# Scatters of edge weights and edge counts spread over more blocks, and paced by the block beside them, in a network of graph and feed-forward layers

## The reference, cut to what matters

```python
# layer 2, graph: a sum weighted by edge_val
h = x @ weight_l
agg = segment_sum(edge_val[:, None] * h[edge_col], edge_row, 3125)
out = agg + bias_l + x @ weight_r + bias_r
# layer 3, graph, twice: a sum with norm = dinv[s] * dinv[d]
h = x @ W
out = segment_sum(h[s] * norm[:, None], d, 3125) + b
```

## Time and profile before

| | us |
|---|---|
| median of 3 timed runs | 4196.15 |
| lowest and highest of them | 4191.04, 4196.79 |
| span of the profiled execution | 4599.8 |

### The profile page before, as it was taken

How to read it: one execution, slowest core, us unless ns; L and a number is a source line. 1 busy time by engine, 2 the same in 40 slices (tenths; PEclk the granted TensorE clock), 3 DMA queues, 4 the chain that set the end, 5 groups by cost and what they waited for, 6 DMA issues and landing times. The chain is left out here.

```text
span 4599.8 us, 50306 instructions
## 1 busy us (share of the span) xinstructions
PE 3306.7 (72%) x14651; PEld 2298.0 (50%) x14651; DVE 1956.1 (43%) x5106; ACT 1198.3 (26%) x3021; POOL 2015.7 (44%) x2028
## 2 busy tenths in 40 slices
PE   3888887177878888348833686798054968999796
PEld 2666665066444455136621454454043744448685
DVE  5554458403666667899833123100044443211201
ACT  2444441023222222148831111000021212103231
POOL 4666656710555555644464554345635421000121
PEclk8666668588888888669966798899576989998898
DMA  4444441002766667147711322543031234332112
GB/s 159 154 161 160 154 166 36 1 1 67 201 194 197 193 192 203 50 141 242 237 58 60 103 88 73 186 150 100 0 124 41 65 96 164 144 108 83 49 37 76
DMA packets 278411, 542.57 MB, mean 118 GB/s; under 512 B 61218, under 2 KB 187110, under 8 KB 277508
## 3 DMA queue, kind: packets, MB, share of 16 engines
q1 hardware_dynamic: 199876, 396.17, 25.5%
q0 software_dynamic: 78272, 143.18, 11.5%
HBM read 370.70 MB, written 168.47 MB: 117 GB/s over the span
## 5 line engine op out<-in xcount | busy, mean ns | idle before, releaser
L1235 PE MATMUL bank<-layer_gnn_h_nodes,layer_gnn_s_onehot_t 128*128 x1664 | 546.3, 456 | 105.1 <-issue 62.7
L144 POOL DMA_INDIRECT edge_weights<-shares,share_cell x416 | 460.2, 1106 | 269.6 <-DMA edge_weights<-shares,share_cell 158.2
L1187 POOL DMA_INDIRECT layer_gnn_s_rows<-gat_rows,src_cols x416 | 401.1, 964 | 370.5 <-DMA kept_rows<-layer_gnn_s_rows 209.7
L134 POOL DMA_INDIRECT edge_counts<-repeats,count_cell x416 | 419.8, 1009 | 270.7 <-DMA edge_counts<-repeats,count_cell 166.0
L496 POOL DMA_INDIRECT layer_gnn_sum_rows<-xn_rows,src_cols x416 | 423.9, 1019 | 199.9 <-issue 102.9
L1235 PEld LDWEIGHTS bank<-layer_gnn_h_nodes,layer_gnn_s_onehot_t 128*128 128x128 f32 x1664 | 316.4, 211 | 201.9 <-issue 127.8
L555 PE MATMUL bank<-layer_gnn_sum_onehot,layer_gnn_sum_rows 128*128 128x128 f32 x1664 | 370.9, 387 | 63.9 <-issue 46.5
L1484 PE MATMUL bank<-layer_gnn_w_onehot,layer_gnn_w_part 128*128 128x128 f32 x1664 | 293.8, 305 | 121.7 <-issue 67.8
L555 PEld LDWEIGHTS bank<-layer_gnn_sum_onehot,layer_gnn_sum_rows 128*128 128x128 f32 x1664 | 322.0, 282 | 116.7 <-issue 81.4
L1484 PEld LDWEIGHTS bank<-layer_gnn_w_onehot,layer_gnn_w_part 128*128 128x128 f32 x1664 | 226.0, 198 | 189.7 <-issue 96.9
L2594 PE MATMUL bank<-layer_gnn_b_weights,xn_nodes 128*128 128x400 f32 x768 | 261.2, 503 | 65.6 <-DMA layer_gnn_b_weights<-edge_weights 65.6
(11 more groups left out here) (611 smaller groups left out, 5565.2 us busy)
## 6 DMA issues: line engine op xcount, KB each, us to landing
kept_rows<-layer_gnn_s_rows SPq DMA_DIRECT2D x104, 512.0 KB
layer_gnn_w_rows<-kept_rows SPq DMA_DIRECT2D x104, 512.0 KB
edge_weights<-layer_gnn_sum_zeros SPq DMA_DIRECT2D x56, 800.0 KB
layer_gnn_b_weights<-edge_weights SPq DMA_DIRECT2D x56, 800.0 KB
layer_gnn_gcn_sum_counts<-edge_counts SPq DMA_DIRECT2D x50, 896.0 KB, 4.4
layer_gnn_s_dst_across<-in_dst_row SPq DMA_DIRECT2D x104, 256.0 KB
edge_counts<-layer_gnn_w_no_edges SPq DMA_DIRECT2D x25, 896.0 KB
layer_ffn_e_w<-in_l1f_w SPq DMA_DIRECT2D x16, 1024.0 KB
```

The lines of the kernel that those rows point to most:

```text
L134: nc.gpsimd.indirect_dma_start(g.counts, bass.IndirectOffsetOnAxis(ap=g.cell[:, t:t + 1].bitcast(U32), axis=0), g.repeats[:, t:t + 1], Non ...
L144: nc.gpsimd.indirect_dma_start(g.weights, bass.IndirectOffsetOnAxis(ap=g.share_cell[:, t:t + 1].bitcast(U32), axis=0), g.shares[:, t:t + 1 ...
L1187: nc.gpsimd.indirect_dma_start(rows[:, t % U, :], None, htable, bass.IndirectOffsetOnAxis(ap=g.srcc[:, t:t + 1].bitcast(U32), axis=0)).the ...
L1235: last = nc.tensor.matmul(g.ps[4 + t % 4][:, 0:D + HEADS], onehot_t[:, t % 4, k, :], hflat[:, ds(w * AW + (k * AW + HEADS), D + HEADS)], s ...
```

## The change

`LANES` becomes 4, and both helpers get a number `ahead`: scatter t waits for t − ahead to have landed. It is 2 as before unless given. A new helper, `place_weights_beside`, also makes each scatter wait for a semaphore of the block: tile t of lo to hi waits until it stands at `first + (t - lo) * steps // (hi - lo)`. The tables become longer.

| block | weights before | weights now | counts before | counts now |
|---|---|---|---|---|
| mod_ffn | 20 + 140 | 20 (one in flight) + 78 paced by `hidden` | | |
| gat_front | | 10 paced by `evicted` | | |
| edge_softmax | 20 | 46 (one in flight) | | |
| weighted_sum | 236 | 190 paced by `summed` | | |
| sw_gate | | 8 (one in flight) | | |
| sw_route | | 10 (one in flight) | 20 | |
| experts, layer 1 | | 54 | 96 | 40 |
| weighted_products | | | 240 | 270 (four in flight) |
| layer2_sums | | | | 20 (one in flight) |
| mo_gate | | | 30 | 16 (one in flight) |
| mo_route | | | 30 | 16 (one in flight) |
| experts, layer 2 | | | | 54, one a tile |

```diff
-LANES = 2
+LANES = 4
...
+def landed(eng, lanes, t):
+
+    eng.wait_ge(lanes[t % LANES], 16 * (t // LANES + 1))
...
+def place_weights(nc, g, pool, lo, hi, ahead=2):
 
     for t in range(lo, hi):
-        lane = g.weights_in[t % LANES]
-        if t >= LANES:
-            pool.wait_ge(lane, 16 * (t // LANES))
+        if t >= ahead:
+            landed(pool, g.weights_in, t - ahead)
         nc.gpsimd.indirect_dma_start(g.weights, bass.IndirectOffsetOnAxis(ap=g.share_cell[:, t:t + 1].bitcast(U32), axis=0),
-                                     g.shares[:, t:t + 1], None).then_inc(lane, 16)
+                                     g.shares[:, t:t + 1], None).then_inc(g.weights_in[t % LANES], 16)
+
+
+def place_weights_beside(nc, g, pool, lo, hi, signal, first, steps):
+
+    for t in range(lo, hi):
+        pool.wait_ge(signal, first + (t - lo) * steps // (hi - lo))
+        place_weights(nc, g, pool, t, t + 1)
...
-PLACED = (160, 180)
-COUNTED = (20, 116, 356, 386)
+PLACED = (20, 98, 108, 154, 344, 352, 362)
+COUNTED = (40, 310, 330, 346, 362)
...
-                place_weights(nc, g, pool, 20, PLACED[0])
+                place_weights_beside(nc, g, pool, PLACED[0], PLACED[1], hidden, 5, NF * (ROWS // G))
...
+                place_weights_beside(nc, g, pool, PLACED[1], PLACED[2], evicted, 1, NT)
...
-            place_weights(nc, g, pool, PLACED[0], PLACED[1])
+            place_weights(nc, g, pool, PLACED[2], PLACED[3], ahead=1)
...
-            place_weights(nc, g, pool, PLACED[1], ET)
+            place_weights_beside(nc, g, pool, PLACED[3], PLACED[4], summed, 1, ET)
...
-                    place_counts(nc, g, pool, COUNTED[0] + per * e, COUNTED[0] + per * (e + 1))
+                    place_weights(nc, g, pool, *share(PLACED[6], ET, e))
+                    place_counts(nc, g, pool, *share(0, COUNTED[0], e))
...
+                    if t < ET - COUNTED[4]:
+                        place_counts(nc, g, pool, COUNTED[4] + t, COUNTED[4] + t + 1)
...
-            place_counts(nc, g, pool, COUNTED[1], COUNTED[2])
+            place_counts(nc, g, pool, COUNTED[0], COUNTED[1], ahead=4)
...
+        @block.gpsimd
+        def _(pool):
+            place_counts(nc, g, pool, COUNTED[1], COUNTED[2], ahead=1)
```

More of the change, by code:

```diff
@@ L125, in _, with place_counts @@
             nc.tensor.matmul(g.ps[0][:, 0:ET], g.ones[0:1, :], df[0:1, :], start=True, stop=True).then_inc(win_sum, 1)
-def place_counts(nc, g, pool, lo, hi):
+def landed(eng, lanes, t):
+    eng.wait_ge(lanes[t % LANES], 16 * (t // LANES + 1))
+def place_counts(nc, g, pool, lo, hi, ahead=2):
     for t in range(lo, hi):
-        lane = g.counts_in[t % LANES]
-        if t >= LANES:
-            pool.wait_ge(lane, 16 * (t // LANES))
+        if t >= ahead:
+            landed(pool, g.counts_in, t - ahead)
         nc.gpsimd.indirect_dma_start(g.counts, bass.IndirectOffsetOnAxis(ap=g.cell[:, t:t + 1].bitcast(U32), axis=0),
-                                     g.repeats[:, t:t + 1], None).then_inc(lane, 16)
-def place_weights(nc, g, pool, lo, hi):
+                                     g.repeats[:, t:t + 1], None).then_inc(g.counts_in[t % LANES], 16)
+def place_weights(nc, g, pool, lo, hi, ahead=2):
     for t in range(lo, hi):
-        lane = g.weights_in[t % LANES]
-        if t >= LANES:
-            pool.wait_ge(lane, 16 * (t // LANES))
+        if t >= ahead:
+            landed(pool, g.weights_in, t - ahead)
         nc.gpsimd.indirect_dma_start(g.weights, bass.IndirectOffsetOnAxis(ap=g.share_cell[:, t:t + 1].bitcast(U32), axis=0),
-                                     g.shares[:, t:t + 1], None).then_inc(lane, 16)
+                                     g.shares[:, t:t + 1], None).then_inc(g.weights_in[t % LANES], 16)
[3 more added lines that the diff above has]
+        place_weights(nc, g, pool, t, t + 1)
 def layer_norm(nc, g, table, meanwhile=None):
@@ L817, in _ @@
                                         pattern=[[-1, P]], channel_multiplier=1).then_inc(passed, 1)
-                place_weights(nc, g, pool, 0, 20)
+                place_weights(nc, g, pool, 0, PLACED[0], ahead=1)
                 for t in range(0, NT):
@@ L2003, in layer1_ffn @@
             norm_gate(nc, g, "sw_gate", wg, [(wg[:, :, :], rows_in(a.l1f_gate_w)), (bg[:, :], a.l1f_gate_b)], bg[0:1, :], logits, g.xn,
-                      zeros[:, :], clear_tiles(r, zeros[:, :]))
-        route(nc, g, "sw_route", logits, 1, CAP, SLOTS, r, g.xn, table, lambda pool: place_counts(nc, g, pool, 0, COUNTED[0]))
+                      zeros[:, :], clear_tiles(r, zeros[:, :]), place=lambda pool: place_weights(nc, g, pool, PLACED[4], PLACED[5], ahead=1))
+        route(nc, g, "sw_route", logits, 1, CAP, SLOTS, r, g.xn, table, lambda pool: place_weights(nc, g, pool, PLACED[5], PLACED[6], ahead=1))
         NF, NR = H1 // P, SLOTS // P
@@ L2141, in _ @@
                 take(1)
-                per = (COUNTED[1] - COUNTED[0]) // E
+                share = lambda lo, hi, e: (lo + (hi - lo) * e // E, lo + (hi - lo) * (e + 1) // E)
                 for e in range(E):
@@ L2186, in layer2_ffn @@
                       flat[:, E * (H2 + D):E * (H2 + D) + D], clear_pads(r, 2, flat[:, E * (H2 + D):E * (H2 + D) + D]), gamma, beta, g_cols, b_cols, load_experts,
-                      lambda pool: place_counts(nc, g, pool, COUNTED[2], COUNTED[3]))
-            route(nc, g, "mo_route", logits, 2, None, None, r, g.acc, table, lambda pool: place_counts(nc, g, pool, COUNTED[3], ET))
+                      lambda pool: place_counts(nc, g, pool, COUNTED[2], COUNTED[3], ahead=1))
+            route(nc, g, "mo_route", logits, 2, None, None, r, g.acc, table, lambda pool: place_counts(nc, g, pool, COUNTED[3], COUNTED[4], ahead=1))
         with ExitStack() as s2:
```

## The result

The changed kernel takes 4072.78 us (median of 4 runs, 4064.83 to 4081.46), the kernel before 4193.59 in the same comparison: ratio 0.9716, 95% interval 0.9700 to 0.9732. The forecast was 4092.

A forecast was written before the change was run, and what follows sets the result against it. POOL's scatters were taken to bound the kernel wherever POOL is last in a block before its barrier. The terms summed to −104.5 us, from 4196 to 4092 us, with a range of 3935 to 4210.

The forecast's parts named there:

- mod_ffn: Block where 140 scatters become 78 paced; PE, not POOL, then ends it: −20 us (bounds −22 and −10).
- edge_softmax: Block where 20 scatters become 46, one in flight at 2.4 us each; POOL ends it: +37 us (bounds +23, +52).
- weighted_sum: Block where 236 scatters become 190, with a pace that never binds; POOL ends sooner: −58 us (bounds −50 and −75).
- weighted_products: Block where 240 scatters become 270, four in flight, 1.3 us each beside loads: −66 us (bounds −74 and −17).
- The sum of the bounds: Whole kernel: all bounds at good ends about 4035 us, all but one rival's at bad ends about 4185.
- what the profiled execution is worth: Step holding that 404 us of the 4599.8 us profiled span are in the profile alone, not in timed runs.
- The count of 395 us: Slow stretches added over four blocks: 142 mod_ffn, 18 weighted_sum, 110 first block, 125 edge_scores; close to the 404 us.
- theory A: PE's slow stretches beside dense scatters and gathers belong to the recording; timed runs go at undisturbed rates; 4092 us, chance 0.55.
- The second rival: Slow stretches real, and four in flight bring them into weighted_products, +141 us there: 4157 to 4240 us, chance 0.10.
- The first rival: Slow stretches real in timed runs and removed by the pace, mod_ffn −162 us: 3950 us, chance 0.13.
- The one on four in flight that only queue: In weighted_products landings queue at the engines, so four in flight don't help: +41 us there, 4199 us, chance 0.09.
- the slower one on landings that come in time: Landings beside loads already timely in timed runs: weighted_sum gains 0, weighted_products +38 us, total 4254 us, chance 0.13.

The follow-up runs named there:

- before_again: The kernel before, unchanged, profiled once more in a single execution on the quick chip: 4177.88 us.
- soft_four: The changed kernel with edge_softmax's 46 scatters four in flight instead of one, on a slow chip: 4637.16 us, ratio 0.9978 to the kernel before.
- no_pace: The changed kernel with the pace undone in mod_ffn, gat_front and weighted_sum, on the quick chip: 4041.77 us, ratio 0.9655 to the kernel before.
- wp_two: The changed kernel with two count scatters in flight in weighted_products instead of four, quick chip: 4185.03 us, ratio 1.0000 to the kernel before.
- b_wp_four: The kernel before with four lanes and four count scatters in flight in weighted_products only, slow chip: 4776.74 us, ratio 1.0284.
- balanced: The changed kernel with four in flight everywhere, no pace, tables set to end POOL just before the others; slow chip: 4941.62 us, ratio 1.0641 to the kernel before.
- ws_four: The changed kernel with edge_softmax back at 20 scatters, weighted_sum with 216, four in flight, unpaced; quick chip: 3944.95 us, ratio 0.9416 to the kernel before.

## Why the prediction was right, and where it was not

For the quick chip the sum was made of the right parts. From the first instruction of a block to the first of the next, in us, before_again against the changed kernel:

| | before | after | change | forecast |
|---|---|---|---|---|
| mod_ffn | 248.7 | 210.5 | −38 | −20 |
| gat_front, edge_scores | 614.0 | 616.2 | +2 | +1.5 |
| edge_softmax | 124.2 | 163.4 | +39 | +37 |
| weighted_sum | 482.0 | 441.4 | −41 | −58 |
| sw_gate, sw_route | 67.6 | 64.4 | −3 | +1.5 |
| experts, layer 1 | 267.7 | 281.5 | +14 | −1 |
| weighted_products | 444.1 | 370.7 | −73 | −66 |
| layer2_sums | 53.3 | 52.5 | −1 | +1 |
| mo_gate, mo_route | 139.4 | 119.7 | −20 | −3 |
| experts, layer 2 | 249.5 | 262.1 | +13 | +2.5 |

They sum to −108 with a forecast of −104.5. Blocks that the change does not touch are 12 us longer in the second trace, so the two traced executions differ by 96 us; the timed medians differ by 121. That the sum comes so close is luck in part: mod_ffn and weighted_sum both lie outside the bounds given for them, by 16 and 9 us, and cancel.

- **mod_ffn** was too small mostly because of the kernel before. The changed block ends where PE's groups end, as worked out, 4 us sooner. But on the quick chip the 140 scatters of before take 194 us, 1.39 each, where the first profile had 1.30, so POOL ended 11 us later than I took it to.
- **edge_softmax** came as forecast, for the reason given, and soft_four confirms it: the price is one in flight.
- **weighted_sum** is the term mis-sized the wrong way. From the block's start to POOL's last scatter it goes from 463 to 434 us, 29 and not 58; the rest of the table's 41 is the wait behind that scatter, 19 us before (a late landing, last section) and 8 now. I wrote that the pace never binds and priced it at nothing; it does not bind, but the second wait costs some 0.2 us a scatter, and 25 us in the block (433.6 to 408.6 in no_pace). A wait that is always fulfilled still has to be executed on the engine that is last.
- **weighted_products** came within 7 us. With four in flight a scatter takes 1.31 us beside the loads (210 in 275), and wp_two gives the 112 us back.
- **experts of layer 1, mo_route, experts of layer 2**: +15, −17 and +10 that no term had. They are late landings, which moved (last section) and, with the −11 of weighted_sum, nearly cancel.
- **The sum of the bounds** was added wrongly at one end: all of them at their bad ends give −1, so 4195 us, not some 4185.

**The step that failed** is the one on what the profiled execution is worth. The count of 395 us came near, and the use made of it was right for the timed runs that it was applied to, that they don't have these slow stretches. Its parts are off: against before_again sum_edges has 83 us where I had 110, edge_scores 181 where I had 125, mod_ffn 131 for 142, and 42 lie in the experts of layer 1, which I left out. Its cause was wrong: they go with the chip (or its hour), not with the one profiled execution. On the three slow chips timed runs have them, and the kernel before needs 4626 to 4663 us; on the quick chip a profile has none. That the forecast holds is luck in this: the same change in a set on a slow chip gives 1.005, which theory A had no room for. I had said that "the profiled span should fall more than the timed runs, towards 4350"; with the profile on the quick chip it fell to 4079.7. The sentences of the Trainium skill that I leaned on ("SBUF — State Buffer", "Who interferes with whom": PE and ACT wait on nobody) can't be the whole account of what a slow chip shows, PE at 125 matmuls in 295 us beside scatters. The Trainium skill ("NOTIFIC — the notification-queue block", section 7.1) names a count of stalls that would mean that the path of the records had throttled an engine; no run here shows that count, and every timed run comes with its span and clock, so none shows the kernel without a recording.

**The second rival is right on the slow chips**, and its price was too small: +187 us in weighted_products (433 to 621), where I had 141. PE does fewer matmuls beside the row than I took from mod_ffn, 158 in 240 us. With mod_ffn's −167 it leaves the kernel at 1.005. The first rival, that the pace alone wins some 250 us, holds on neither kind: it does win mod_ffn's 167 on a slow chip, and the four in flight lose it again. The one on four in flight that only queue, and the slower one on landings that come in time, fell with wp_two (on the quick chip). A reader who wants one number for the change must say for which chip: 0.972 or 1.005.

What stays open: what makes a chip slow, whether it stays so, and what the engines wait for in a dense row. That the loads stall with the engines, and that 1.8 us a scatter does no harm while rows at 1.3 do (ten in gat_front excepted), is all that the runs say.

## What to carry to other kernels

Before a profile is subtracted from a timed run, see that both come from the same chip and the same set: two blocks that a change can't touch, here 76 and 179 us apart, are the sign. Where POOL ends a block behind scatters that wait for their landings, more in flight is the cheap cure on the quick chip (112 us for one number), but on the slow chips rows of indirect DMAs 1.3 us apart hold every engine up (the same number costs 130 us there, b_wp_four); 1.8 us apart they do not, and a pace by the block's own progress with four in flight gave 0.952 there, where the change itself gave 1.005. On the quick chip that kernel was not measured. And a second semaphore wait before each scatter, on the engine that is last, cost some 0.2 us each, even though it was always fulfilled.

## What the runs showed of the hardware that was not expected

- Four chips, one set of runs on each, fall into two kinds, 10 to 11% apart in the same kernel. Most of the difference lies in the blocks with dense indirect DMAs: over all traces sum_edges takes 554 to 562 us against 638 to 650, edge_scores 559 to 561 against 719 to 757, and mod_ffn as it was before 244 against 375 to 384.
- A landing is now and then some 15 to 19 us late, with no packet starting meanwhile, and whoever waits for it then pays. In before_again it is the barriers behind weighted_sum and mo_route (POOL's last scatter at 2074.97, the next block at 2094.90), in the changed kernel a scatter in the experts of layer 1. The row of POOL in each:

```profile
2094.90 1.80 POOL L1839 MEMSET layer_ffn_zero_rows<- 128x2048 f32 x1 [18.97 <-POOLq L3100]
```

```profile
2392.61 0.96 POOL L138 DMA_INDIRECT edge_counts<-repeats,count_cell  x1 [15.66 <-DMA edge_counts<-repeats,count_cell]
```

In the first profile the same 20 us stood behind POOL's last scatter of weighted_sum (2462.5 to 2482.7). PE's and DVE's tail ended at 2480.8 beside them, and I read them as that alone. Both traces of the kernel before have it at the 1248th indirect DMA. The changed kernel and the seven runs made from it that keep its order (all but balanced), on quick and slow chips, have one in the experts of layer 1, where POOL waits 15 to 16 us before the 1346th. So it follows the order of indirect DMAs, not chance; what it is in that order stays open.
- Beside loads at a DMA share of 0.75 four in flight bring a scatter to 1.54 us (ws_four), at a share of 0.53 to 1.31 (the changed kernel).
